# Two width-16 attentions: rounds of two pairs, four heads' scores on four strips, projection pieces in two slots a round

## The chip, the core and the metric

The kernel is one program on one core of a Trainium2 chip. The metric is the device time of one launch in microseconds, of which the median of three runs is given. TensorE (PE) multiplies, with its weight loads as PEld; VectorE (DVE), ScalarE (ACT) and GpSimd (POOL) compute; SyncE (SP) issues the transfers. The engines run side by side, each in its own fixed order, and wait for one another at semaphores.

## What is computed

Eight layers run after one another over x of 8 batches, 112 rows and 256 columns. The fifth and the seventh are the attentions of this change. Both have 16 heads of width 16 and 375 keys from the same context:

```python
# layer 5 (a2): _L2_xattn_ref
logits = jnp.einsum('bhqd,bhkd->bhqk', q, k) / jnp.sqrt(jnp.asarray(dh, q.dtype))
neg = (1.0 - mask.astype(q.dtype)) * -1000000000.0
attn = jax.nn.softmax(logits + neg[:, None, :, :], axis=-1)
attn = attn * group_prob[:, None, :, :]
out = jnp.einsum('bhqk,bhkd->bhqd', attn, v)     # then out @ wo_k + wo_b
# layer 7 (a3): _L3_xattn_ref
scores = jnp.einsum('bhqd,bhkd->bhqk', qh, kh) * SCALE
attn = jax.nn.softmax(scores, axis=-1)
out = jnp.einsum('bhqk,bhkd->bhqd', attn, vh)    # then out @ Wo.T + bo
# both: x = x + tanh(g) * attention(layernorm(x), ctx)
```

## The kernel before

Both layers are `narrow_attention`; a2 is called with `group` and `mask`, a3 without them and with `spare`, a helper that prepares the last layer's weights on idle engines. The 16 heads of a batch are eight pairs, numbered n = 8b + k over all eight batches b, so n runs from 0 to 63.

For each pair, TensorE makes the scores (`scores`), VectorE the negated maximum (`maximum`), ScalarE the exponents and their sum (`exponent`). In a2 GpSimd multiplies by the group (`regroup`). TensorE transposes the two probabilities (`turn`, two halves in banks 4 and 5), ScalarE copies the first half and VectorE the second (`copy_turned`), and for every two pairs TensorE multiplies with v (`weigh`, bank 6). The reciprocal of the sums (`invert`), its spreading to 128 columns on GpSimd (`expand`), TensorE's transpose of it (piece "I"), ScalarE's copy (`spread`) and VectorE's product (`move_out`) finish eight heads.

A head's scores use a strip of 32 of the array's 128 rows and a PSUM bank of their own, number j for strip j. A pair takes strips and banks 0 and 1 if n is even, 2 and 3 if odd. So the scores of pair n + 1 can be made while pair n is being read. Each score is three matmuls (high by high, high by low, low by high parts).

Between these steps TensorE makes the projections of the next batch, cut into pieces that all go to bank 7: K twice, V twice (twelve matmuls, then six), I twice and O once (the output projection of the batch before) for each batch, and Q at two places in all. The table `later` says after which n a piece stands, and `bank_free` makes it wait until the piece before it has been taken out of bank 7: K, V and O by VectorE (`evacuate`), I by ScalarE (`spread`), Q by both.

The order on every engine is written out by hand: one loop over n on each. Two other chains cross them. `high_context` (ScalarE) and `low_context` (GpSimd) split the context of batch b + 2 into parts before its K pieces; `high_queries` and `low_queries` do so with the queries of batch b + 1 before its first scores. GpSimd's loop is `regroup` for each n with these between.

## Time and profile before

| | us |
|---|---|
| median of three runs | 1427.72 |
| lowest, highest | 1417.14, 1428.33 |
| the profiled execution | 1423.97 |
| its span, first to last instruction | 1422.2 |
| TensorE busy in it | 1204.7 (85%) |
| VectorE, ScalarE, GpSimd busy | 860.9, 672.9, 532.3 |
| mean granted TensorE clock | 0.928 |

The profile is one execution. Busy shares over the whole span mix eight layers with different limits; for this change the stretches of the two attentions count. The steps before the first scores and after the last transpose stand outside them.

### The profile page before, as it was taken

The numbers are of one execution on the slowest core, as the hardware profiler recorded it, in microseconds if no ns is written. First come the engines' busy times: TensorE is split into PE (matmuls) and PEld (weight loads), VectorE is DVE, ScalarE is ACT, GpSimd is POOL, SyncE is SP. The second block draws the span as 40 slices with busy tenths as digits, with TensorE's granted clock in tenths as the row PEclk, the third lists the DMA queues.
The fourth block names the chain that finished last, engine by engine and source line by source line (L and its number), as shares of the span: only waits on it lengthen the run. The fifth ranks groups of instructions, "written<-read, shape, count | busy, mean of one in ns | idle before, by whom it ended". The sixth has DMA issues, their size and how long they took to land. (4 is left out here: it accounts for less than half of the span.)

```text
span 1422.2 us, 25398 instructions
## 1 busy us (share of the span) xinstructions
PE 1204.7 (85%) x9539; PEld 951.9 (67%) x9539; DVE 860.9 (61%) x1950; ACT 672.9 (47%) x1518; POOL 532.3 (37%) x537
## 2 busy tenths in 40 slices
PE   2999999999996887679999638999999428999967
PEld 2677777777774355456777538998888426777634
DVE  6664565555543336557787447667676356777686
ACT  3345543554541321256666316545554016766665
POOL 3355554565543000267887522001100232162132
PEclk9999999999997988779999559999999858999998
DMA  6000000000001052301100335565652152000000
GB/s 177 11 3 12 12 1 12 12 1 1 1 1 22 0 159 59 85 5 42 35 31 11 115 111 190 181 204 182 197 177 102 52 169 53 23 12 3 1 7 21
DMA packets 59929, 88.63 MB, mean 62 GB/s; under 512 B 8640, under 2 KB 49808, under 8 KB 59808
## 3 DMA queue, kind: packets, MB, share of 16 engines
q1 hardware_dynamic: 57696, 81.49, 18.5%
q0 software_dynamic: 2112, 5.51, 1.3%
q8 instruction: 78, 1.28, 0.4%
q14 instruction: 43, 0.35, 0.1%
HBM read 81.48 MB, written 5.51 MB: 61 GB/s over the span
## 5 line engine op out<-in xcount | busy, mean ns | idle before, releaser
L906 POOL TENSOR_SCALAR a_arena<-a_arena 112x487 f32<-112x487 f32 x128 | 192.7, 1517 | 175.3 <-DVE a_arena L1117 175.3
L1198 ACT ACTIVATE a_arena<-banks,a_arena 112x487 f32<-112x487 f32 x128 | 84.2, 663 | 192.1 <-DVE a_arena L1111 192.1
L1111 DVE TENSOR_REDUCE a_arena<-banks 112x2 f32<-112x974 f32 x64 | 75.0, 1172 | 101.1 <-PE banks L997 101.1
L93 PE MATMUL banks<-f_x_high,f_up_high 128*128 128x256 f32 x448 | 128.3, 286 | 3.6 <-DVE f_up_low L1981 2.2
L94 PE MATMUL banks<-f_x_low,f_up_high 128*128 128x256 f32 x448 | 127.9, 286 | 0.0
L95 PE MATMUL banks<-f_x_high,f_up_low 128*128 128x256 f32 x448 | 127.8, 285 | 0.0
L397 POOL TENSOR_TENSOR a_arena<-a_arena 112x375 f32<-112x375 f32 x128 | 114.7, 922 | 26.9 <-ACT a_arena L704 26.8
L513 PE MATMUL banks<-ident,a_arena 112*126 112x112 f32 x768 | 106.9, 277 | 12.0 <-POOL a_arena L397 10.0
L513 PEld LDWEIGHTS banks<-ident,a_arena 112*126 112x126 f32 x768 | 78.4, 145 | 46.6 <-issue 26.4
L2018 POOL DMA_INDIRECT f_arena<-f_rows,f_arena x28 | 32.1, 1145 | 194.7 <-PE banks L2051 175.2
L2162 DVE TENSOR_TENSOR f_arena<-banks,f_arena 128x512 f32<-128x512 f32 x56 | 38.5, 688 | 100.4 <-ACT f_arena L2141 100.4
L712 ACT COPY a_arena<-banks 126x336 f32<-126x336 f32 x128 | 55.9, 437 | 75.6 <-PE banks L513 75.6
L93 PEld LDWEIGHTS banks<-f_x_high,f_up_high 128*128 128x128 f32 x448 | 87.2, 195 | 4.2 <-issue 2.4
L93 PE MATMUL banks<-a_wv_high,a_kvT_high 128*122 128x512 f32 (+1 forms) x224 | 85.1, 380 | 4.8 <-DVE a_wv_low L605 2.9
L94 PEld LDWEIGHTS banks<-f_x_low,f_up_high 128*128 128x128 f32 x448 | 87.2, 195 | 0.0
L95 PEld LDWEIGHTS banks<-f_x_high,f_up_low 128*128 128x128 f32 x448 | 87.2, 195 | 0.0
L93 PE MATMUL banks<-a_kvT_high,a_wk_high 128*128 128x488 f32 (+1 forms) x192 | 82.7, 431 | 3.7 <-POOL a_kvT_low L891 3.5
L93 PE MATMUL banks<-f_down_high,f_h_high 128*128 128x256 f32 x224 | 64.4, 287 | 22.5 <-DVE f_arena L2175 22.5
L704 ACT ACTIVATE a_arena<-a_arena 112x375 f32<-112x375 f32 x128 | 77.0, 605 | 2.3 <-DVE a_arena L620 2.2
L95 PE MATMUL banks<-a_wv_high,a_kvT_low 128*122 128x512 f32 (+1 forms) x224 | 77.3, 345 | 0.0
L94 PE MATMUL banks<-a_wv_low,a_kvT_high 128*122 128x512 f32 (+1 forms) x224 | 77.3, 345 | 0.0
L704 ACT ACTIVATE a_arena<-banks,a_arena 112x375 f32<-112x375 f32 x128 | 72.8, 579 | 8.4 <-DVE a_arena L623 7.8
(331 smaller groups left out, 3312.6 us busy)
## 6 DMA issues: line engine op xcount, KB each, us to landing
f_arena<-in_L_ffn_w1T SPq DMA_DIRECT2D x14, 1024.0 KB, 5.8
f_arena<-in_L_ffn_w3T SPq DMA_DIRECT2D x14, 1024.0 KB, 4.8
f_arena<-in_L_ffn_w2T SPq DMA_DIRECT2D x14, 1024.0 KB
a_arena<-in_ctxT SPq DMA_DIRECT2D x24, 375.0 KB, 4.6
a_arena<-in_ctx SPq DMA_DIRECT2D x16, 375.0 KB
f_y<-f_arena SPq DMA_DIRECT2D x14, 256.0 KB, 5.0
a_arena<-in_L_xattn_Wkv SPq DMA_DIRECT2D x2, 1024.0 KB, 9.9
a_arena<-in_fside_BxSxS SPq DMA_DIRECT2D x8, 164.1 KB, 2.4
```

Of the source, the lines that this page charges most:

```text
L93: pe.matmul(out, sh, mh, start=start, stop=False)
L94: pe.matmul(out, sh, ml, start=False, stop=False)
L95: return pe.matmul(out, sl, mh, start=False, stop=stop)
L397: op = pool.tensor_tensor(z, z, gp[u], ALU.mult)
L513: mm = pe.transpose(psT[s][0:SZ, c * T:(c + 1) * T], prob[n % 4 * 2 + s][:, SZ * c:SZ * c + SZ], ident[0:T, 0:T])
L704: act.activation(prob[n % 4 * 2 + s][:, 0:KEYS], src, ACT.Exp, bias=negmax[:, n % 4, s:s + 1], scale=-1.0 if grouped else 1.0, accum_out=t ...
L712: act.copy(probT[n % 4 * 2].rearrange("k c t -> k (c t)"), psT[0][0:SZ, 0:NC * T]).then_inc(copied0, 1)
L906: pool.tensor_scalar(z, z, inv[:, n % 4, s:s + 1], None, ALU.mult).then_inc(p_ready, 1)
L1111: dve.tensor_reduce(negmax[:, n % 4, :], banks[0:T, 0:2, 0:KEYS], AX, ALU.max, negate=True).then_inc(max_ready, 1)
L1198: act.activation(prob[n % PR][s][:, 0:KEYS], banks[0:T, s, 0:KEYS], ACT.Exp, bias=negmax[:, n % 4, s:s + 1], accum_out=total[:, n % 4, s:s ...
L2018: pool.indirect_dma_start(rows[k % 2][:, h, :], None, rows_dram, bass.IndirectOffsetOnAxis(routing.token[:, h, k:k + 1], 0)).then_inc(rows ...
L2162: dve.tensor_tensor(gated[n % 2], ps3[n % 3], gel[n % 2], ALU.mult).then_inc(gated_done, 1)
```

## The change

Scores are made for two pairs (four heads) at once, on all four strips and banks: `scores(q)` for the pairs 2q and 2q + 1. Every loop goes in steps of two pairs, a round. On TensorE a round is: `turn` of the pair before, scores of the next round, a piece in the first slot, `turn`, `weigh`, a piece in the second slot. `scores` waits until all four maxima of the round before are there. VectorE, ScalarE and GpSimd are reordered to match. In a3 the maximum is made as in a2, with a `neg` of zeros, and the exponents read its result in SBUF, no longer the banks. K stands at k = 0 and 2 (before: 2 and 3), Q at n = 11 and 19 (before 8 and 16), `low_queries` at k = 4 (before 3); the spare work starts four pairs later.

```diff
--- before.py
+++ after.py
@@ -250,16 +250,16 @@
...
-    later = {8: ("Q", 0, 1), 16: ("Q", 1, 1)}
+    later = {11: ("Q", 0, 1), 19: ("Q", 1, 1)}
     for b in range(B):
         if b + 1 < B:
-            for k, kind, arg in ((2, "K", 0), (3, "K", 1), (6, "V", 0), (7, "V", 1)):
+            for k, kind, arg in ((0 if b else 3, "K", 0), (2 if b else 4, "K", 1), (6, "V", 0), (7, "V", 1)):
                 later[8 * b + k] = (kind, arg, b + 1)
...
     if spare is not None:
-        later[24] = ("M", 0, 0)
+        later[27] = ("M", 0, 0)
...
+        else:
+            neg = [m.sb("neg", [T, KEYS])] * 2
+        scored = [m.sb(f"scored{j}", [T, KEYS]) for j in range(4)]
+        spacers = m.sb("spacers", [T, 4])
...
+            else:
+                pool.memset(neg[0], 0.0).then_inc(neg_made, 1)
...
             pool.tensor_tensor(x[:], x[:], obs.unsqueeze(1).to_broadcast([T, B, D]), ALU.add).then_inc(biased, 1)
             for n in range(PAIRS + 2):
                 b, k = n // STEPS, n % STEPS
+                if n >= 4 and n % 4 == 0:
+                    expand(n // 4 - 1)
                 if grouped and n < PAIRS:
                     regroup(n)
-                if n >= 4 and n % 4 == 0:
-                    expand(n // 4 - 1)
                 if k == 1 and grouped and b + 1 < B:
                     negate_mask(b + 1)
                 if k == 5 and b + 2 < B:
                     low_context(b + 2)
-                if k == 3 and b + 1 < B:
+                if k == 4 and b + 1 < B:
                     low_queries(pool, b + 1)
-                if spare is not None and 26 <= n < 26 + spare.STEPS // 2:
+                if spare is not None and 30 <= n < 30 + spare.STEPS // 2:
                     for j in range(2):
-                        spare.gpsimd(pool, 2 * (n - 26) + j)
+                        spare.gpsimd(pool, 2 * (n - 30) + j)
...
-            def scores(n):
-                b, i, s = n // STEPS, n // 2 % 4, n % 2
-                u, g, e = b % 2, i // 2, i % 2
-                if n % STEPS == 0:
+            def scores(q):
+                b, g, e = q // 4, q // 2 % 2, q % 2
+                u = b % 2
+                if q % 4 == 0:
                     pe.wait_ge(piece_moved, moved(("K", 1, b))[0])
-                if n % STEPS == 0:
                     pe.wait_ge(q_low, b + 1)
-                if n > 1:
-
-                    pe.wait_ge(max_ready if grouped else exp_done, 2 * (n - 1))
+                if q:
+
+                    pe.wait_ge(max_ready, 4 * q)
                 for k, (a, z) in enumerate(((0, 0), (0, 1), (1, 0))):
-                    for h, j in heads_of(n):
+                    for j in range(4):
                         r = slice(32 * j, 32 * j + 32)
...
-            scores(1)
-            for n in range(LAST):
+            for n in range(0, LAST, 2):
+                if 0 < n <= PAIRS:
+                    turn(n - 1)
                 if n + 2 < PAIRS:
-                    scores(n + 2)
-                if n < PAIRS:
-                    turn(n)
-                if n >= 3 and n % 2 and n < PAIRS + 2:
-                    weigh((n - 3) // 2)
+                    scores(n // 2 + 1)
                 if n in later:
                     bank_free(n)
                     piece(later[n], 7)
+                if n < PAIRS:
+                    turn(n)
+                if 2 <= n < PAIRS + 2:
+                    weigh(n // 2 - 1)
+                if n + 1 in later:
+                    bank_free(n + 1)
+                    piece(later[n + 1], 7)
...
-                dve.wait_ge(s_ready, n + 1)
-                j, r = 2 * (n % 2), n % 4
...
-                else:
-                    dve.tensor_reduce(negmax[:, r, :], banks[0:T, j:j + 2, 0:KEYS], AX, ALU.max,
-                                      negate=True).then_inc(max_ready, 2)
+                dve.wait_ge(s_ready, n // 2 + 1)
+                b, j, r = n // STEPS, 2 * (n % 2), n % 4
+                if n % STEPS == 0 and (grouped or b == 0):
+                    dve.wait_ge(neg_made, b + 1)
+                if n > 1:
+                    dve.wait_ge(exp_done, 2 * (n - 1))
+                for s in range(2):
+
+                    dve.memset(spacers[:, j + s:j + s + 1], 0.0)
+                    dve.tensor_tensor_reduce(scored[j + s], banks[0:T, j + s, 0:KEYS], neg[b % 2], -1.0, LARGEST,
+                                             ALU.add, ALU.min, negmax[:, r, s:s + 1]).then_inc(max_ready, 1)
...
+            def taken(n):
+                if n in later and later[n][0] != "I":
+                    evacuate(later[n], 7)
+                    if later[n][0] == "O":
+                        dve.wait_ge(piece_moved, moved(later[n])[0])
+                        follow.row(dve, later[n][2])
+
             maximum(0)
-            for n in range(LAST + 1):
-                if n + 1 < PAIRS:
-                    maximum(n + 1)
+            maximum(1)
+            for n in range(0, LAST + 1, 2):
                 if 0 < n <= PAIRS:
                     copy_turned(n - 1)
-                if n >= 4 and n % 4 == 0 and n <= PAIRS:
-                    invert(n // 4 - 1)
+                taken(n - 1)
+                if n % 4 == 2 and n < PAIRS:
+                    invert(n // 4)
+                if n + 2 < PAIRS:
+                    maximum(n + 2)
                 if n >= 6 and n % 4 == 2 and n <= PAIRS + 2:
                     move_out(n // 4 - 1)
-                if n - 1 in later and later[n - 1][0] != "I":
-                    evacuate(later[n - 1], 7)
-                    if later[n - 1][0] == "O":
-                        dve.wait_ge(piece_moved, moved(later[n - 1])[0])
-                        follow.row(dve, later[n - 1][2])
+                taken(n)
+                if n < PAIRS:
+                    copy_turned(n)
+                if n + 3 < PAIRS:
+                    maximum(n + 3)
...
-                    act.wait_ge(max_ready, 2 * n + s + 1 if grouped else 2 * n + 2)
+                    act.wait_ge(max_ready, 2 * n + s + 1)
                     if n > 3:
                         act.wait_ge(t_ready, 2 * (n - 4) + s + 1)
-                    src = scored[j][:, 0:KEYS] if grouped else banks[0:T, j, 0:KEYS]
-                    act.activation(prob[n % 4 * 2 + s][:, 0:KEYS], src, ACT.Exp, bias=negmax[:, n % 4, s:s + 1],
-                                   scale=-1.0 if grouped else 1.0, accum_out=total[:, b % 2, h:h + 1]
+                    act.activation(prob[n % 4 * 2 + s][:, 0:KEYS], scored[j], ACT.Exp, bias=negmax[:, n % 4, s:s + 1],
+                                   scale=-1.0, accum_out=total[:, b % 2, h:h + 1]
...
-            for n in range(LAST + 1):
-                if n < PAIRS:
-                    exponent(n)
-                if spare is not None and n in (6, 9, 12, 14):
-                    spare.scalar(act, (6, 9, 12, 14).index(n))
+            exponent(0)
+            exponent(1)
+            for n in range(0, LAST + 1, 2):
                 if 0 < n <= PAIRS:
                     copy_turned(n - 1)
                 if n >= 6 and n % 4 == 2 and n <= PAIRS + 2:
                     spread(n // 4 - 1)
+                if n - 1 in later and later[n - 1][0] == "Q":
+                    odd(later[n - 1], 7)
+                if n + 2 < PAIRS:
+                    exponent(n + 2)
+                if n < PAIRS:
+                    copy_turned(n)
+                if n + 3 < PAIRS:
+                    exponent(n + 3)
+                if spare is not None and n in (6, 8, 12, 14):
+                    spare.scalar(act, (6, 8, 12, 14).index(n))
                 if n % STEPS == 4 and n // STEPS + 2 < B:
                     high_context(n // STEPS + 2)
-                if n - 1 in later and later[n - 1][0] == "Q":
-                    odd(later[n - 1], 7)
                 if n % STEPS == 2 and n // STEPS + 1 < B:
                     high_queries(n // STEPS + 1)
```

TensorE in a2 around the O piece of batch 2 (L466, L470), at k = 4 and after. L497 (L500 in the changed kernel) is `scores`, L513 (L516) `turn`, L532 (L535) `weigh`, L460 (L464) piece I, L93 here the first matmul of V. Before:

```order
L513 MATMUL banks<-ident,a_arena 126x112 x6
L466 MATMUL banks<-a_arena 112x256 x2
L497 MATMUL banks<-a_kT_high,a_q_high 112x376 x2
L497 MATMUL banks<-a_kT_low,a_q_high 112x376 x2
L497 MATMUL banks<-a_kT_high,a_q_low 112x376 x2
L513 MATMUL banks<-ident,a_arena 126x112 x6
L532 MATMUL banks<-a_arena 32x112 x12
L460 MATMUL banks<-ident,a_arena 128x112
L497 MATMUL banks<-a_kT_high,a_q_high 112x376 x2
L497 MATMUL banks<-a_kT_low,a_q_high 112x376 x2
L497 MATMUL banks<-a_kT_high,a_q_low 112x376 x2
L513 MATMUL banks<-ident,a_arena 126x112 x6
```

After:

```order
L500 MATMUL banks<-a_kT_high,a_q_high 112x376 x4
L500 MATMUL banks<-a_kT_low,a_q_high 112x376 x4
L500 MATMUL banks<-a_kT_high,a_q_low 112x376 x4
L470 MATMUL banks<-a_arena 112x256 x2
L516 MATMUL banks<-ident,a_arena 126x112 x6
L535 MATMUL banks<-a_arena 32x112 x12
L464 MATMUL banks<-ident,a_arena 128x112
L516 MATMUL banks<-ident,a_arena 126x112 x6
L500 MATMUL banks<-a_kT_high,a_q_high 112x376 x4
L500 MATMUL banks<-a_kT_low,a_q_high 112x376 x4
L500 MATMUL banks<-a_kT_high,a_q_low 112x376 x4
L93 MATMUL banks<-a_wv_high,a_kvT_high 126x256
```

Four heads stand in each score row, and between two score blocks there are two transposes and both slots. The V piece follows the scores directly, with I as the piece before it.

ScalarE in a2, batch 2, from k = 4 on. L704 (L714) is `exponent`, L712 (L722) `copy_turned`, L688 (L699) `high_context`, L733 (L743) `spread`, L729 the second half of Q. Before:

```order
L704 ACTIVATE a_arena<-a_arena 112x375 x2
L712 COPY a_arena<-banks 126x336
L688 CAST a_kvT_high<-a_arena 128x2x375
L704 ACTIVATE a_arena<-a_arena 112x375 x2
L712 COPY a_arena<-banks 126x336
L704 ACTIVATE a_arena<-a_arena 112x375 x2
L712 COPY a_arena<-banks 126x336
L733 COPY a_arena<-banks 128x112
```

After:

```order
L722 COPY a_arena<-banks 126x336
L729 ACTIVATE a_arena<-banks,a_arena 128x448
L714 ACTIVATE a_arena<-a_arena 112x375 x2
L722 COPY a_arena<-banks 126x336
L714 ACTIVATE a_arena<-a_arena 112x375 x2
L699 CAST a_kvT_high<-a_arena 128x2x375
L722 COPY a_arena<-banks 126x336
L743 COPY a_arena<-banks 128x112
L714 ACTIVATE a_arena<-a_arena 112x375 x2
```

Before, `high_context` stands between the exponents of k = 4 and k = 5, and `spread` behind the exponents of k = 6. Now both stand behind the exponents of k = 7, with a copy between them.

GpSimd in a2, batch 4, from k = 2 on. L397 (L399) is `regroup`, L363 (L365) `low_queries`, L388 (L390) `expand`, L371 (L373) `low_context`. Before:

```order
L397 TENSOR_TENSOR a_arena<-a_arena 112x375 x4
L363 TENSOR_TENSOR a_q_low<-a_arena,a_q_high 128x448
L397 TENSOR_TENSOR a_arena<-a_arena 112x375 x2
L388 COPY a_arena<-a_arena 112x128
L397 TENSOR_TENSOR a_arena<-a_arena 112x375 x2
L371 TENSOR_TENSOR a_kvT_low<-a_arena,a_kvT_high 128x2x375
L397 TENSOR_TENSOR a_arena<-a_arena 112x375 x6
```

After:

```order
L399 TENSOR_TENSOR a_arena<-a_arena 112x375 x4
L390 COPY a_arena<-a_arena 112x128
L399 TENSOR_TENSOR a_arena<-a_arena 112x375 x2
L365 TENSOR_TENSOR a_q_low<-a_arena,a_q_high 128x448
L399 TENSOR_TENSOR a_arena<-a_arena 112x375 x2
L373 TENSOR_TENSOR a_kvT_low<-a_arena,a_kvT_high 128x2x375
L399 TENSOR_TENSOR a_arena<-a_arena 112x375 x4
```

`expand` moved ahead of the products of k = 4, `low_queries` behind them; `low_context` stands behind those of k = 5 as before.

## Rows read from the trace of the kernel before

**Rows 1.** Busy us of each engine (and instructions) in stretches; then granted clock.
```profile
616.90:630.70 13.80, 8.65 (x38) 6.75 (x40) 4.77 (x21) 6.22 (x20) 12.84 (x13) 0.51 0.01 1
727.50:748.40 20.90, 20.76 (x233) 15.74 (x232) 16.61 (x71) 14.53 (x45) 17.82 (x22) 1.00 0.12 37
780.90:787.70 6.80, 6.80 (x48) 4.81 (x50) 2.44 (x12) 3.31 (x11) 4.80 (x7) 0.50 0.00 0
1285.20:1305.90 20.70, 20.70 (x233) 15.71 (x232) 15.85 (x31) 14.24 (x45) 3.21 (x4) 1.00 0.01 3
```

**Rows 2.** Timeline of TensorE in one batch of a2: start, length, engine, line.
```profile
706.68 0.36 PE L93 MATMUL banks<-a_wv_high,a_kvT_high 128*126 128x256 f32 x1
...
708.26 0.43 PE L497 MATMUL banks<-a_kT_high,a_q_high 32*112 32x376 f32 x2
...
715.96 0.79 PE L513 MATMUL banks<-ident,a_arena 112*126 112x112 f32 x6
716.52 0.42 PE L93 MATMUL banks<-a_kvT_high,a_wk_high 128*128 128x376 f32 x1
...
717.74 0.42 PE L497 MATMUL banks<-a_kT_high,a_q_high 32*112 32x376 f32 x2
...
722.70 1.12 PE L466 MATMUL banks<-a_arena 128*112 128x256 f32 x4
723.75 0.43 PE L497 MATMUL banks<-a_kT_high,a_q_high 32*112 32x376 f32 x2
...
724.45 0.79 PE L513 MATMUL banks<-ident,a_arena 112*126 112x112 f32 x6
725.18 0.78 PE L532 MATMUL banks<-a_arena 126*32 126x112 f32 x24
725.89 0.47 PE L460 MATMUL banks<-ident,a_arena 112*128 112x112 f32 x2
726.29 0.42 PE L497 MATMUL banks<-a_kT_high,a_q_high 32*112 32x376 f32 x2
```

**Rows 3.** Timeline of TensorE at the first scores of a3.
```profile
1176.90 0.44 PE L497 MATMUL banks<-a_kT_high,a_q_high 32*112 32x376 f32 x4
```

**Rows 4.** Timeline of VectorE in the same batch as rows 2.
```profile
716.08 0.55 DVE L620 CUSTOM_DVE_ANT_0 a_arena<-banks,a_arena 112x375 f32<-112x375 f32 x1 [0.15 <-issue]
...
717.02 0.50 DVE L630 COPY a_arena<-banks 126x336 f32<-126x336 f32 x1
717.84 0.61 DVE L580 TENSOR_SCALAR a_kT_high<-banks,a_arena 128x376 fp32r<-128x376 f32 x1 [0.32 <-PE banks L95]
...
719.02 0.55 DVE L620 CUSTOM_DVE_ANT_0 a_arena<-banks,a_arena 112x375 f32<-112x375 f32 x1
...
723.52 0.50 DVE L630 COPY a_arena<-banks 126x336 f32<-126x336 f32 x1
723.94 0.47 DVE L599 SCALAR_TENSOR_TENSOR x<-banks,tanh_g,x 112x256 f32<-112x256 f32 x1
```

**Rows 5.** Timeline of ScalarE in the same batch.
```profile
715.36 0.25 ACT L733 COPY a_arena<-banks 128x112 f32<-128x112 f32 x1 [0.87 <-PE banks L460]
715.51 0.57 ACT L727 CAST a_q_high<-a_arena 128x448 fp32r<-128x448 f32 x1
...
719.16 0.44 ACT L712 COPY a_arena<-banks 126x336 f32<-126x336 f32 x1 [0.38 <-PE banks L513]
719.50 0.82 ACT L688 CAST a_kvT_high<-a_arena 128x750 fp32r<-128x750 f32 x1
720.21 0.61 ACT L704 ACTIVATE a_arena<-a_arena 112x375 f32<-112x375 f32 x1
```

**Rows 6.** Timeline of GpSimd in the same batch.
```profile
718.50 1.16 POOL L363 TENSOR_TENSOR a_q_low<-a_arena,a_q_high 128x448 fp32r<-128x448 f32 x1
719.60 1.81 POOL L397 TENSOR_TENSOR a_arena<-a_arena 112x375 f32<-112x375 f32 x2
...
723.34 1.79 POOL L371 TENSOR_TENSOR a_kvT_low<-a_arena,a_kvT_high 128x750 fp32r<-128x750 f32 x1
```

More of the change, by code:

```diff
@@ L297, in narrow_attention @@
             neg = [m.sb(f"neg{u}", [T, KEYS]) for u in range(2)]
-            scored = [m.sb(f"scored{j}", [T, KEYS]) for j in range(4)]
-            spacers = m.sb("spacers", [T, 4])
+        else:
+            neg = [m.sb("neg", [T, KEYS])] * 2
+        scored = [m.sb(f"scored{j}", [T, KEYS]) for j in range(4)]
+        spacers = m.sb("spacers", [T, 4])
         psT, psO, psP = [banks[:, 4 + j, :] for j in range(2)], banks[:, 6, :], banks[:, 7, :]
@@ L608, in maximum @@
             def maximum(n):
-                dve.wait_ge(s_ready, n + 1)
-                j, r = 2 * (n % 2), n % 4
-                if grouped:
-                    b = n // STEPS
-                    if n % STEPS == 0:
-                        dve.wait_ge(neg_made, b + 1)
-                    if n > 1:
-                        dve.wait_ge(exp_done, 2 * (n - 1))
-                    for s in range(2):
-                        dve.memset(spacers[:, j + s:j + s + 1], 0.0)
-                        dve.tensor_tensor_reduce(scored[j + s], banks[0:T, j + s, 0:KEYS], neg[b % 2], -1.0, LARGEST,
-                                                 ALU.add, ALU.min, negmax[:, r, s:s + 1]).then_inc(max_ready, 1)
-                else:
-                    dve.tensor_reduce(negmax[:, r, :], banks[0:T, j:j + 2, 0:KEYS], AX, ALU.max,
-                                      negate=True).then_inc(max_ready, 2)
+                dve.wait_ge(s_ready, n // 2 + 1)
[8 more added lines that the diff above has]
+                                             ALU.add, ALU.min, negmax[:, r, s:s + 1]).then_inc(max_ready, 1)
             def copy_turned(n):
@@ L725, in high_queries @@
                 if b > 1:
-                    act.wait_ge(s_ready, STEPS * (b - 1))
+                    act.wait_ge(s_ready, STEPS // 2 * (b - 1))
                 act.copy(q_parts[b % 2][0][:], qm[:, :, :, b * T:(b + 1) * T]).then_inc(q_high, 1)
```

## Prediction

> **What bounds the kernel now.** I read the stretches first, then the order on TensorE inside one batch, then the other engines over the same microseconds. The change touches only the two width-16 attentions, called a2 (with group and mask) and a3 below. They run from about 614 and 1177 us. A middle batch of a2 lasts 20.90 us, of which TensorE is busy 20.76. One of a3 lasts 20.70 and TensorE never idles in it [rows 1]. So TensorE is the bound, and a block taken off its queue is worth its full length until another engine becomes the bound. The reader should look at that second candidate in the same rows: GpSimd is busy 17.82 us of a batch in a2, VectorE 16.61 (a2) and 15.85 (a3), ScalarE 14.53 and 14.24. The gap above the next engine is only 3 us.
>
> By starts on TensorE [rows 2]: a score block S (three passes, two heads) takes 0.70 us, the transposes of a pair T 0.73, the weighing W of two pairs 0.71, pieces K 1.22, V (twelve matmuls) 1.58, O 1.05, I 0.40; V with six matmuls I put at 0.9. A T before K is 0.56, before W 0.73: what follows in another shape of the array costs some 0.15 more. K and V were followed by S and are now followed by T, so I take 0.15 off each of them: K 1.07, V 1.43 and 0.75. Before, a batch is 8 S, 8 T, 4 W and seven pieces.
>
> **What is removed.** Four heads now share one S. Do four strips cost more than two? At the head of a3 the first two score blocks already follow each other with nothing between, and the trace merges them: a pass over four strips is 0.44 us against 0.42 for two [rows 2, 3]. So four S of 0.70 leave each batch: 2.8 us. 31 rounds in each of two attentions have a block to drop, some 62 x 0.70 = 43 us. That is what the change would give if nothing else held TensorE.
>
> The Trainium skill ("TensorE: Matmul & The Clock Gate", Measured speedup vs the span model) gives four row strips a speedup of 3.07, not 4, that is 1.3 times the time of one strip. By that, about 0.15 us would be added to each of the 62 rounds, 9 us in all. The row on four strips disagrees, and the row decides.
>
> **What is added: one set of score banks.** Before, S for the next pair went to two banks while VectorE read the other two. Now S takes all four, so it waits until both maxima of the round before are done. I lay out one round from the start of S at 0, with VectorE in its new order: maximum, evacuation of the piece, copy of T, maximum.
> - First maximum starts 0.82 after S; a pair of maxima takes 0.94; a K piece is taken up 1.32 after its start and costs 1.18; a copy 0.42 [rows 4].
> - Round with K and no delay: maxima to 1.76, K (started at 0.70) taken up at 2.02, done 3.20, copy 3.62, maxima 4.56, and with 0.14 for the last maximum's accumulator and the signal (an estimate) S at 4.70. TensorE alone would need 0.70 + 1.07 + 0.73 + 0.71 + 0.73 = 3.94. VectorE is the bound there.
> - Round with O and I: TensorE 0.70 + 1.05 + 0.73 + 0.71 + 0.40 + 0.73 = 4.32, VectorE 4.2. Round with both V: TensorE 0.70 + 1.43 + 0.73 + 0.71 + 0.75 + 0.73 = 5.05.
> Sum 4.70 + 4.70 + 4.32 + 5.05 = 18.8 against 20.8. So a third of what the blocks and shapes save already goes to VectorE's chain.
>
> The Trainium skill ("TensorEngine Tiling (Array Packing)", PSUM Bottleneck) warns of this: tiling speeds up the matmuls, not the emptying of PSUM, which can take over. By that rule alone a batch would end near 18.8; the round with K agrees with it, the V round does not.
>
> **What is moved: ScalarE and the one piece bank.** All pieces use bank 7, so a piece waits until the one before has been taken out. I is now in the second slot of a round (k = 1 and 5) and K or V in the first slot of the next (k = 2 and 6). I is taken out by ScalarE (`spread`), which now stands behind the two exponents of the pair whose maximum came last, and behind a copy. An exponent costs 0.61, a copy 0.34, `spread` 0.25 [rows 5]. Last maxima start 1.08 before S; first exponent 0.58 later, two take 1.22, copy 0.34, `spread` 0.25: bank 7 is free 1.33 after S, where the piece could go at 0.70.
> - Round k = 2: K starts at 1.33 instead of 0.70, VectorE takes it up at 2.65, then 1.18, 0.42 and 1.08 for the next S: 5.3 instead of 4.7.
> - Round k = 6: in the new order `high_context` (0.71, [rows 5]) also stands ahead of that copy and `spread`, so V starts at 2.04: 2.04 + 1.43 + 0.73 + 0.71 + 0.75 + 0.73 = 6.4 instead of 5.05.
> - Round k = 0: V's second half is taken out only after the copy of T, so K starts some 0.25 late: 4.9.
> Sum 4.9 + 5.3 + 4.3 + 6.4 = 20.9 in a3, against 20.7: +0.2. The score blocks saved are waited for again.
>
> **a2 has GpSimd too.** It multiplies each probability (`regroup`, 1.81 a pair), and T waits for it. `low_queries` (1.16) now stands behind `regroup` of k = 4 and needs ScalarE's `high_queries`, which comes after the exponents of pair k = 5. GpSimd is through with k = 4 about 2 us before that, and waits. `low_context` (1.79 [rows 6]) stands behind `regroup` of k = 5 and needs `high_context`, now behind the exponents of k = 7: another 1.5 us of waiting. Add 3.5 to the 17.8 it is busy and GpSimd needs 21.3, more than TensorE had. Laid out: T of k = 5 waits 0.6, T of k = 6 waits 1.3 behind `low_context`, and the other waits of these rounds partly overlap: about 22.3 us a batch against 20.9, +1.4.
>
> **The small parts.** In the first batch the clock is half (0.51 in [rows 1]) and a score block costs about 1.2, so dropping two there is worth more: -2.0 in a3; in a2 GpSimd's late start and `low_context` keep all but 0.5. Batch 6 has no `high_context`: -0.5 in each. Batch 7 has no K or V; a round of 3.55 before stays near 3.6 by ScalarE and VectorE, and only its O round gains: -0.8 in each. In a3 the maximum is now two instructions, 0.94 a pair, in place of one reduction of about the same, already in the layout. The new `memset` of `neg` lies ahead of the first scores beside a GpSimd that waits: nothing. The Q pieces move one slot and the spare weight work four pairs later; I cost both at zero, because the spare work only needs to end before a3 does; between -1 and +1 a batch for the two batches with Q.
>
> **Sum.** a2: 5 x 1.4 - 0.5 - 0.5 - 0.8 = +5.2. a3: 5 x 0.2 - 2.0 - 0.5 - 0.8 = -2.3. Together +3 us on the profiled execution, 1423.97, so 1427. The median of the runs shown is 3.75 above that execution: 1430.7, and I say 1430. About 1% (14 us) is what a measurement of this kernel can tell from no change. An error of 0.7 us in one batch's layout repeats 14 times and makes 10 us, so 1418 to 1442 is this case's own range.
>
> **Rivals.**
> *Only VectorE's chain binds (faster).* If ScalarE runs early enough that bank 7 is free when asked for, and GpSimd never waits long, a batch is 18.8: 12 x 2.0 + 3 at the ends = -27 from the median, 1401. For it: ScalarE has 6 us of slack a batch and GpSimd 3. Against it: their order, in which the wanted copy stands behind exponents that are released last. 0.28, of which 0.03 for the whole 43 us (1385).
>
> **Chances.** Forecast's case 0.50, faster 0.28, slower 0.22. The range takes in the faster rival's 1401 and half of the slower one: 1396 to 1452.
>
> **What would show it.** Score rows with x4 and a pass near 0.44: removed work right. TensorE waits before K at k = 2 and before V at k = 6, of 0.6 and 1.3 us, released by ScalarE's copy of I: the bank. S waiting on VectorE's maximum in K rounds: the chain. In a2, T waiting for GpSimd's product, with GpSimd idle until ScalarE's two casts. Batches of 20.9 in a3 and 22.3 in a2. I am wrong if a batch of a3 is below 20, if a2's batches are not longer than a3's, or if the clock falls inside the middle batches.

## The result, and the profile after

The changed kernel took 1441.08 us (median of 10 runs, 1432.09 to 1446.03), the kernel before, on the same chip, 1424.88 (10 runs, 1415.70 to 1437.97). The ratio is 1.0116, 95% interval 1.0087 to 1.0145: slower by 16 us. The range (1396 to 1452) holds it. The forecast was 1430, that is 0.2% above the median that it started from; the measured time is inside its own band of 1418 to 1442 by only 0.9 us, and as a ratio it is slower by more than the 1% that the forecast's case allowed. The profiled execution took 1440.02.

The head of the profile of the changed kernel: its span, then the busy time of the engines.

```profile
span 1438.3 us, 25718 instructions
PE 1166.2 (81%) x9539; PEld 929.8 (65%) x9539; DVE 865.9 (60%) x2270; ACT 676.5 (47%) x1518; POOL 532.1 (37%) x538
```

TensorE is busy 38.5 us less than before, and the span is 16.1 us longer. (Between the second profiles of both kernels, experiments 9 and 10, it is 46.1 us; 43 were predicted.) So the work was removed, and TensorE waits for more than it saved. One batch of a2, one of a3, and 3.4 us inside a3's second batch, columns as in [rows 1]:

```profile
684.17:706.91 22.74, 18.42 (x230) 14.16 (x230) 16.12 (x70) 14.40 (x44) 18.08 (x22) 1.00 0.12 34
1275.15:1296.26 21.11, 18.07 (x231) 14.16 (x231) 16.62 (x71) 14.46 (x45) 15.56 (x19) 1.00 0.07 20
1215.50:1218.90 3.40, 3.29 (x12) 2.93 (x12) 1.24 (x3) 1.69 (x6) 0.00 (x0) 0.50 0.00 0
```

In [rows 1] TensorE idled 0.14 us of a batch of a2 and not at all in a3. Now it idles 4.3 and 3.0. No other engine is full either, so these are waits in a circle of engines. The timeline of TensorE in that batch of a3 shows them: start, length, and in brackets the idle time ahead and who ended it.

```profile
1279.53 0.43 PE L500 MATMUL banks<-a_kT_high,a_q_high 32*112 32x376 f32 x4
...
1280.54 0.45 PE L93 MATMUL banks<-a_kvT_high,a_wk_high 128*128 128x376 f32 x1 [0.23 <-DVE a_arena L597]
...
1284.58 0.43 PE L500 MATMUL banks<-a_kT_high,a_q_high 32*112 32x376 f32 x4 [0.32 <-DVE a_arena L625]
...
1285.90 0.44 PE L93 MATMUL banks<-a_kvT_high,a_wk_high 128*128 128x376 f32 x1 [0.55 <-ACT a_arena L743]
...
1289.93 0.43 PE L500 MATMUL banks<-a_kT_high,a_q_high 32*112 32x376 f32 x4 [0.39 <-DVE a_arena L625]
...
1294.31 0.43 PE L500 MATMUL banks<-a_kT_high,a_q_high 32*112 32x376 f32 x4 [0.20 <-DVE a_arena L625]
...
1296.26 0.38 PE L93 MATMUL banks<-a_wv_high,a_kvT_high 128*126 128x256 f32 x1 [1.17 <-ACT a_arena L743]
```

Each of these score rows is x4 and 0.43 long, as [rows 3], and a whole block of four strips takes 0.70 by starts, as one of two strips did. K follows the scores by 1.01 and 1.32, V by 1.95 us, where 0.70 would do. The last two are released by L743, `spread`. ScalarE over the last of these waits:

```profile
1293.72 0.61 ACT L714 ACTIVATE a_arena<-a_arena 112x375 f32<-112x375 f32 x1 [0.70 <-DVE a_arena L625]
...
1294.33 0.59 ACT L714 ACTIVATE a_arena<-a_arena 112x375 f32<-112x375 f32 x1
...
1294.92 0.80 ACT L699 CAST a_kvT_high<-a_arena 128x750 fp32r<-128x750 f32 x1
1295.63 0.43 ACT L722 COPY a_arena<-banks 126x336 f32<-126x336 f32 x1
1295.96 0.25 ACT L743 COPY a_arena<-banks 128x112 f32<-128x112 f32 x1
```

Two exponents, `high_context` (L699), a copy and then `spread`, which frees bank 7. In a2 the same cast holds up GpSimd, which waits 1.66 us for it and only then multiplies the pair whose transpose TensorE is waiting for. GpSimd first, then TensorE:

```profile
728.93 1.80 POOL L373 TENSOR_TENSOR a_kvT_low<-a_arena,a_kvT_high 128x750 fp32r<-128x750 f32 x1 [1.66 <-ACT a_kvT_high L699]
730.69 1.78 POOL L399 TENSOR_TENSOR a_arena<-a_arena 112x375 f32<-112x375 f32 x2
```

```profile
727.33 0.80 PE L516 MATMUL banks<-ident,a_arena 112*126 112x112 f32 x6 [0.66 <-POOL a_arena L399]
...
732.53 0.79 PE L516 MATMUL banks<-ident,a_arena 112*126 112x112 f32 x6 [1.43 <-POOL a_arena L399]
```

A batch is measured from its first V matmul to that of the next batch. The first stretch starts at the first scores, the last one ends at the start of the last O matmul. The profiled executions compare so (us; "predicted" is the prediction's difference):

| | before | after | difference | predicted |
|---|---|---|---|---|
| a2, to the first V | 25.61 | 25.25 | -0.4 | -0.5 |
| a2, two batches with Q | 46.31 | 50.16 | +3.9 | +2.8 |
| a2, three middle batches | 62.60 | 67.95 | +5.4 | +4.2 |
| a2, batch 6 | 20.89 | 21.87 | +1.0 | -0.5 |
| a2, end | 29.38 | 27.67 | -1.7 | -0.8 |
| a3, to the first V | 21.87 | 22.02 | +0.2 | -2.0 |
| a3, two batches with Q | 44.98 | 50.23 | +5.3 | +0.4 |
| a3, three middle batches | 62.15 | 63.24 | +1.1 | +0.6 |
| a3, batch 6 | 20.68 | 20.39 | -0.3 | -0.5 |
| a3, end | 23.12 | 23.61 | +0.5 | -0.8 |
| both attentions | 357.6 | 372.4 | +14.8 | +2.9 |

The unchanged layers make up the rest of 16.1.

One row of the table can't be taken at its word. The end of a2 holds 11.0 us at half clock in the profile before and 9.4 in the one after. In experiments 8 and 9, which run the old function there, it holds 3.4 and takes 25.95 and 25.94, not 29.38. The profile before, that of experiment 9, and the changed kernel:

```profile
769.30:798.68 29.38, 25.90 (x275) 19.07 (x273) 15.84 (x71) 14.49 (x47) 18.08 (x22) 0.81 0.00 1
```

```profile
765.28:791.22 25.94, 22.46 (x274) 17.07 (x273) 15.99 (x71) 14.49 (x47) 18.07 (x22) 0.93 0.00 1
```

```profile
773.99:801.66 27.67, 22.41 (x276) 17.26 (x272) 16.89 (x73) 14.27 (x45) 18.42 (x23) 0.83 0.00 1
```

The changed kernel takes 27.67 there in both its profiles. So its end of a2 is 1.7 us shorter against one profile of the kernel before and 1.7 longer against the other.

### The profile page after: what moved, and what is told of

The parts are those of the page before. It is cut to its first block and busy times, and to the rows that moved or that the text cites. A ratio compares the mean times of both kernels' runs of the same rounds, so it can differ in the third digit from the quotient of the medians.

```text
span 1438.3 us, 25718 instructions
## 1 busy us (share of the span) xinstructions
PE 1166.2 (81%) x9539; PEld 929.8 (65%) x9539; DVE 865.9 (60%) x2270; ACT 676.5 (47%) x1518; POOL 532.1 (37%) x538
## 5 line engine op out<-in xcount | busy, mean ns | idle before, releaser
L714 ACT ACTIVATE a_arena<-a_arena 112x375 f32<-112x375 f32 x256 | 153.8, 602 | 92.8 <-DVE a_arena L625 90.6
L625 DVE CUSTOM_DVE_ANT_0 a_arena<-banks,a_arena 112x375 f32<-112x375 f32 x256 | 130.8, 546 | 8.7 <-issue 5.3
L93 PE MATMUL banks<-f_x_high,f_up_high 128*128 128x256 f32 x448 | 128.6, 287 | 3.6 <-DVE f_up_low L1997 2.2
L516 PE MATMUL banks<-ident,a_arena 112*126 112x112 f32 x768 | 103.7, 272 | 21.3 <-POOL a_arena L399 13.7
L399 POOL TENSOR_TENSOR a_arena<-a_arena 112x375 f32<-112x375 f32 x128 | 114.1, 919 | 5.5 <-ACT a_arena L714 4.5
L516 PEld LDWEIGHTS banks<-ident,a_arena 112*126 112x126 f32 x768 | 84.7, 147 | 37.2 <-POOL a_arena L399 19.2
L93 PE MATMUL banks<-a_wv_high,a_kvT_high 128*122 128x512 f32 (+1 forms) x224 | 86.0, 384 | 18.7 <-ACT a_arena L743 13.7
L2178 DVE TENSOR_TENSOR f_arena<-banks,f_arena 128x512 f32<-128x512 f32 x56 | 38.5, 688 | 103.0 <-ACT f_arena L2157 103.0
L93 PE MATMUL banks<-a_kvT_high,a_wk_high 128*128 128x488 f32 (+1 forms) x192 | 83.8, 436 | 16.6 <-ACT a_arena L743 7.6
L93 PEld LDWEIGHTS banks<-f_x_high,f_up_high 128*128 128x128 f32 x448 | 87.6, 195 | 4.2 <-issue 2.4
L632 DVE COPY a_arena<-banks 126x336 f32<-126x336 f32 x128 | 64.2, 501 | 43.1 <-PE banks L516 43.1
L93 PE MATMUL banks<-f_down_high,f_h_high 128*128 128x256 f32 x224 | 65.4, 292 | 22.5 <-DVE f_arena L2191 22.5
```

Of the source, the lines that this page charges most:

```text
L93: pe.matmul(out, sh, mh, start=start, stop=False)
L399: op = pool.tensor_tensor(z, z, gp[u], ALU.mult)
L516: mm = pe.transpose(psT[s][0:SZ, c * T:(c + 1) * T], prob[n % 4 * 2 + s][:, SZ * c:SZ * c + SZ], ident[0:T, 0:T])
L625: dve.tensor_tensor_reduce(scored[j + s], banks[0:T, j + s, 0:KEYS], neg[b % 2], -1.0, LARGEST, ALU.add, ALU.min, negmax[:, r, s:s + 1]).t ...
L632: dve.tensor_copy(probT[n % 4 * 2 + 1].rearrange("k c t -> k (c t)"), psT[1][0:SZ, 0:NC * T]).then_inc(copied1, 1)
L714: act.activation(prob[n % 4 * 2 + s][:, 0:KEYS], scored[j], ACT.Exp, bias=negmax[:, n % 4, s:s + 1], scale=-1.0, accum_out=total[:, b % 2, ...
```

## The experiments

Ratios are to the kernel before on the same chip. Batch lengths are from the V piece of one batch to that of the next, as above; "Q" marks the two with a Q piece.

**1. Piece I in a bank of its own.** I goes to unused columns of bank 6; K and V wait only for pieces that VectorE takes out.

```diff
-                    mm = pe.matmul(ps[:, 0:T], invx[gg % 2], ident[0:T, 0:T], start=True, stop=True)
+                    if gg:
+                        pe.wait_ge(i_moved, gg)
+                    mm = pe.matmul(psI, invx[gg % 2], ident[0:T, 0:T], start=True, stop=True)
...
-                before = [later[j] for j in sorted(later) if j < n]
+                if later[n][0] == "I":
+                    return
+                before = [later[j] for j in sorted(later) if j < n and later[j][0] != "I"]
...
-                act.copy(iT, psP[:, 0:T]).then_inc(i_moved, 1)
+                act.copy(iT, psI).then_inc(i_moved, 1)
```

> The changed kernel, with piece I written beside the weighing's output in bank 6 and so no longer in bank 7: no K or V piece waits for ScalarE's copy of I. My theory (the waits for bank 7 eat the gain): TensorE's wait before K at k = 2 (0.6 us) and before V at k = 6 (1.25 us) are gone. a3's batches go from 21.07 to about 19.0 us, a2's from 22.7 to about 21.5, since there low_context still comes late: 20 to 25 us less than the changed kernel, a ratio to the kernel before of about 0.995 to 1.0. Rival, VectorE's chain alone binds: the K round stays at 5.3 and only the V round gains, at most 9 us. Rival, the clock: the time stays at 1.012.

Measured: 1430.62 us, ratio 1.0052 (1.0016 to 1.0087). a3's middle batches take 19.26 to 19.57, so the bank was worth 1.8 us a batch there (1.5 in the last of the three). In a2 the expectation (21.5) was missed: they take 24.19, 23.12 and 22.20. The first two hold 3.4 us at half clock each; the third, at full clock, is 0.5 shorter than in the changed kernel. TensorE reaches the transpose sooner and waits longer for GpSimd, 1.81 in the second of them and in the first 2.69, where it was 1.43:

```profile
691.08 0.80 PE L519 MATMUL banks<-ident,a_arena 112*126 112x112 f32 x6 [2.69 <-POOL a_arena L400]
```

So in a2 GpSimd, and what GpSimd waits for, leaves little of this gain. The ratio was expected at 0.995 to 1.0 and came out above.

**2. Both casts early.** `high_context` and `high_queries` stand ahead of the exponents of the next pair.

```diff
                     odd(later[n - 1], 7)
+                if n % STEPS == 4 and n // STEPS + 2 < B:
+                    high_context(n // STEPS + 2)
+                if n % STEPS == 2 and n // STEPS + 1 < B:
+                    high_queries(n // STEPS + 1)
                 if n + 2 < PAIRS:
                     exponent(n + 2)
...
-                if n % STEPS == 4 and n // STEPS + 2 < B:
-                    high_context(n // STEPS + 2)
-                if n % STEPS == 2 and n // STEPS + 1 < B:
-                    high_queries(n // STEPS + 1)
```

> The changed kernel, with high_context and high_queries on ScalarE moved ahead of the exponents of their round instead of behind them. My theory: V at k = 6 starts 1.3 after its scores instead of 1.94, in a3 0.6 us less a batch; in a2 GpSimd's low_context and low_queries no longer wait, and the transposes at k = 5 and k = 6 with them: 1.5 us less a batch. About 4 + 10 = 14 us less than the changed kernel, ratio to before about 1.002. If only VectorE's chain or the clock count, nothing changes (1.012).

Measured: 1423.23 us, ratio 0.9985 (0.9950 to 1.0019). Middle batches are 20.35 in both attentions: 0.7 less in a3 (0.6 expected) and 2.3 less in a2 (1.5 expected). In the middle batches the two attentions become equal once GpSimd need not wait.

**3. Both edits.**

> Both edits: I in bank 6 and the two ScalarE casts ahead of the exponents. My theory: what is left is VectorE's chain in the K rounds. Batches of 18.8 to 19.2 in a3 and 19.0 to 19.8 in a2, 35 to 40 us less than the changed kernel, ratio to before 0.985 to 0.99. If VectorE's chain alone had been the cause, this is no better than 1.005.

Measured: 1404.23 us, ratio 0.9858 (0.9801 to 0.9916). All middle batches are 19.27, within 0.02. Together the two give more than their sum: 36.9 us off the changed kernel, against 10.5 and 17.9 by the medians, and 37, 9 and 19 by the ratios. The traces show two reasons for it, without dividing it between them: in a2 the first edit alone shortens a batch by 0.5 and no more, and with it alone five of the six batches of a2 between V pieces hold 3.4 us at half clock, with both none.

**4. VectorE's maxima first.** The changed kernel, with `maximum(n + 3)` ahead of the pieces and the copy.

```diff
+                if n + 3 < PAIRS:
+                    maximum(n + 3)
                 if n >= 6 and n % 4 == 2 and n <= PAIRS + 2:
                     move_out(n // 4 - 1)
-                taken(n)
                 if n < PAIRS:
                     copy_turned(n)
-                if n + 3 < PAIRS:
-                    maximum(n + 3)
+                taken(n)
```

> The changed kernel, with VectorE making both maxima of a round one after the other, ahead of the copy of the first transposes and of taking out the piece. The scores' wait for VectorE is gone from the K rounds. Rival (VectorE's chain alone binds): a batch falls by 0.6 + 1.2 and the kernel by 25 us, to 0.994 of the kernel before. My theory: the exponents come earlier too, so ScalarE reaches its copy of I before or just after the scores and the bank waits shrink as well; the piece is taken out of bank 7 some 1.4 us later and the next piece waits for that. 15 to 30 us less. It alone can't tell the two theories apart; e1 does.

Measured: 1435.97 us, ratio 1.0102 (1.0063 to 1.0141). The scores no longer wait for VectorE, but the pieces do, since they are taken out of bank 7 later:

```profile
1298.05 0.47 PE L464 MATMUL banks<-ident,a_arena 112*128 112x112 f32 x2 [1.05 <-DVE a_kT_low L589]
...
1307.29 0.47 PE L464 MATMUL banks<-ident,a_arena 112*128 112x112 f32 x2 [0.57 <-DVE x L606]
```

The last two middle batches of a3 gain 0.4 us, those of a2 0.4 to 0.5, and the first of a3 loses 0.9. Expected were 15 to 30 us; 5 came, by the medians, with intervals of the ratios that overlap. VectorE's chain is one side of the circle, bank 7 another; to loosen one alone moves the wait.

**5. All three edits.**

> I in bank 6, the two ScalarE casts early, and both maxima first on VectorE in every round. My theory of what is left in e3 (a batch of 19.27 in both attentions): scores wait 0.5 to 0.7 us for VectorE in the two K rounds. Here these waits go, but the pieces are taken out later, and the next piece waits for bank 7 (V's second half for its first by 0.6 us, more at k = 0): about 18.8 to 19.6 a batch, a ratio of 0.983 to 0.99. If VectorE's chain is not what is left, nothing changes or the batch gets longer.

Measured: 1404.38 us, ratio 0.9852 (0.9770 to 0.9934). Middle batches 18.82 (19.95 in the one of a3 that holds the spare piece M), 0.45 better than in experiment 3, but those with Q 22.6 instead of 21.5 to 22.0, and nothing is left of it in the time.

**6. Experiment 3 with the maxima first only where a K piece stands.** In rounds with O or V the order of the changed kernel stays; before k = 0 the second V piece is taken out ahead of the copy.

```diff
+                early = later.get(n, "K")[0] == "K"
+                if early and n + 3 < PAIRS:
+                    maximum(n + 3)
...
-                taken(n)
+                if not early:
+                    taken(n)
                 if n < PAIRS:
                     copy_turned(n)
-                if n + 3 < PAIRS:
+                if early:
+                    taken(n)
+                elif n + 3 < PAIRS:
                     maximum(n + 3)
```

> As e3, with both maxima first only in the rounds whose first piece is K, and V's second half taken out ahead of the copy of the transposes at k = 0. My theory: the waits of the scores (0.5 and 0.7 us) and of K at k = 0 (0.3 us) go, and a batch is 18.0 to 18.6, 10 to 17 us less than e3: ratio 0.975 to 0.98. If the chain is bound by VectorE's total work instead (16.6 us busy in 19.27), it stays within 3 us of e3.

Measured: 1402.70 us, ratio 0.9836 (0.9734 to 0.9939). Two middle batches, columns as before:

```profile
714.47:732.76 18.29, 17.44 (x234) 14.23 (x231) 16.52 (x70) 14.35 (x46) 17.10 (x21) 1.00 0.15 42
1264.96:1283.22 18.26, 17.40 (x235) 14.23 (x231) 16.47 (x70) 14.36 (x46) 10.86 (x12) 1.00 0.01 3
```

TensorE idles 0.9 us of a batch. The layout was met in the middle batches (18.0 to 18.6 expected; 19.46 in the one with M), the time was not: 10 to 17 us less than experiment 3 were expected, and it is 1.5 less. The batches between V pieces together are 5.6 us shorter; those with Q are 22.0, up to 0.5 longer than in experiment 3. The rest is inside the spread of executions, 1393.57 to 1410.57 here.

**7. Only `high_context` early.**

> The changed kernel with high_context alone moved ahead of the exponents; high_queries stays late. It splits e2. My theory: in a3 the same as e2, 20.4 a batch, since only high_context stands ahead of the copy of I at k = 6. In a2 the wait of the transposes at k = 6 (1.3 us, behind low_context) goes, the one at k = 5 (0.5 to 0.8 us, behind low_queries) stays: 21.0 a batch against 20.35 in e2 and 22.7 in the changed kernel. Ratio to before about 1.002.

Measured: 1420.55 us, ratio 0.9972 (0.9932 to 1.0012). a3's middle batches 20.35, a2's 20.44 to 21.07 (20.4 and 21.0 expected). This one cast accounts for nearly all of experiment 2: 1.7 to 2.3 us of a batch in a2 and 0.7 in a3.

**8. The change in a3 alone.** a2 keeps the function of before.

> The change in a3 alone; a2 runs the function of before. My theory, from the traces: a2 lost 10 us and a3 6, so this is 6 to 7 us slower than before, 1.0045, and a2's part is larger because only there does GpSimd stand between exponents and transposes. If the loss comes from anything that both share (bank 7, the maxima), the two halves are equal, 1.006.

Measured: 1433.38 us, ratio 1.0050 (1.0012 to 1.0087). Its interval is too wide to tell the expectation's two cases, 1.0045 and 1.006, apart. By the first two profiles a3 lost 6.7 us of the 14.8 and a2 8.1. Both attentions lose time; how it divides stays open, since the end of a2 alone moves by 3.4 between profiles (above).

**9 and 10. The kernel before and the changed one once more,** one execution each, for the spread of the layers that nothing changed.

> The kernel before once more, for a second profile of it. From a3's last scores to the end the first profile has 80.7 us and every kernel with the change 86 to 92, of which the last layer, whose code is the same, makes 4 us or more at a half clock. If the change causes that, this profile has 80 to 82 again; if it is the spread between executions, 84 to 90.

> The changed kernel once more, for the same purpose. The batches stay at 22.5 and 21.1 us (order and waits are fixed); the part after a3's last scores is again between 86 and 92 if the change causes it, and anywhere from 80 to 92 if it does not.

Measured: 1431.71 and 1439.32 us. After the last O of a3 the kernel before takes 72.5 us in the first profile and 79.7 in this one:

```profile
1349.70:1422.20 72.50, 50.54 (x226) 30.91 (x224) 54.88 (x140) 44.17 (x66) 22.22 (x25) 0.88 0.05 14
```

```profile
1349.90:1429.60 79.70, 54.80 (x227) 32.39 (x225) 54.93 (x140) 44.28 (x66) 22.16 (x25) 0.80 0.04 12
```

VectorE's and ScalarE's work is the same within 0.2 us, the granted clock 0.88 and 0.80. The changed kernel takes 77.0 and 77.1, between the two. (Counted from the last scores, as the expectation does, it is 80.7 and 87.8 before, 88.0 and 88.1 after.) So the last layer's longer time is no effect of the change. The two attentions together take 357.6 and 355.5 us before, 372.4 and 376.5 after: 14.8 to 21.0 more, in line with the 16 of the medians. So the loss lies inside the attentions, as far as two profiles of each kernel can tell.

**11. The spare Abs behind the copy of I.**

```diff
                     odd(later[n - 1], 7)
+                if spare is not None and n in (8, 10, 14, 16):
+                    spare.scalar(act, (8, 10, 14, 16).index(n))
...
-                if spare is not None and n in (6, 8, 12, 14):
-                    spare.scalar(act, (6, 8, 12, 14).index(n))
```

> The changed kernel with one move on ScalarE in a3: the four Abs instructions of the spare work (1.04 us and 0.19 each) stand behind the copy of I and the second half of Q of the next round, not behind the exponents ahead of them. In the changed kernel one ends just before the copy that frees bank 7 at n = 10 and another before the one at n = 14, and the first Q batch of a3 takes 24.7 to 25.3 us at full clock, the second 22.7 to 23.4. If those Abs are what makes the first one long, K at n = 10 starts 0.5 to 0.7 after the scores end instead of 1.6, V at n = 14 1.2 instead of 2.2, and the first Q batch falls to 22.7 to 23.4. If Q itself makes it long, it stays at 24.7 or more. The whole time should fall by 1 to 2 us, less than one execution can show.

Measured: 1440.52 us, one execution. In the changed kernel an Abs of 1.04 stood just ahead of the copy and `spread`, and K waited 1.59 (the V after it 2.21):

```profile
1213.96 1.04 ACT L2268 ACTIVATE qw_arena<-qw_arena 128x1024 bf16<-128x1024 f32 x1
...
1215.00 0.42 ACT L722 COPY a_arena<-banks 126x336 f32<-126x336 f32 x1
1215.32 0.24 ACT L743 COPY a_arena<-banks 128x112 f32<-128x112 f32 x1
```

```profile
1215.61 0.68 PE L93 MATMUL banks<-a_kvT_high,a_wk_high 128*128 128x376 f32 x1 [1.59 <-ACT a_arena L743]
```

Here the same K and the V after it wait no longer than in a middle batch:

```profile
1211.09 0.44 PE L93 MATMUL banks<-a_kvT_high,a_wk_high 128*128 128x376 f32 x1 [0.55 <-ACT a_arena L743]
...
1223.72 0.39 PE L93 MATMUL banks<-a_wv_high,a_kvT_high 128*126 128x256 f32 x1 [1.18 <-ACT a_arena L743]
```

The first Q batch is 24.89 us with 3.4 of them at half clock, against 26.81 with as many in the changed kernel. At full clock it would be near 23.4 (an estimate from the 1.55 us that such a stretch cost in experiment 10, below), as the second one is (23.42). So the Abs made it 1.9 longer. Experiment 2 agrees: with the Abs in its old place its two Q batches in a3, both at full clock, are 24.72 and 22.70.

**12. Experiment 6 with the Abs moved.**

> The kernel of the sixth experiment (piece I in bank 6, both context casts early, maximum first in K rounds) with the four Abs moved as in the eleventh. There no piece waits for the copy of I, so the Abs only delay a copy of T. If bank 7 was the whole of their cost, nothing changes: the first Q batch of a3 stays at 22.0, as a2's, and the ratio is 0.984 again. If a late copy of T costs too, it falls by up to 1 us. Either way within 0.980 to 0.988.

Measured: 1404.74 us, ratio 0.9879 (0.9852 to 0.9906). The Q batches stay at 22.0. Where no piece waits for the copy of I, the place of the Abs costs nothing. The layouts of experiments 3, 5, 6 and 12 all end between 1402.7 and 1404.7 us, 1.2 to 1.6% below the kernel before; their intervals overlap and none of them can be called best.

## Why the prediction was right or wrong

**Right: TensorE was the bound, four strips cost as two.** The x4 rows, the block of 0.70 and the 38.5 us less of busy time show it. The rival of strips that don't overlap falls.

**Right: the waits and their makers.** K at k = 0, K at k = 2 and V at k = 6 were put at 0.95, 1.33 and 2.04 behind the scores, and came at 1.01, 1.32 and 1.95. A middle batch of a3 was put at 20.9 and took 21.1. In a2 the transpose of k = 5 was to wait 0.6 and that of k = 6 1.3; they wait 0.66 and 1.43, and a middle batch takes 22.5 to 22.7 against 22.3. Experiment 1 shows the cause in a3 (the piece that ScalarE holds in bank 7), experiments 2 and 7 the one in a2 (the casts behind the exponents), and experiment 3 that with both undone the kernel is faster than before. The 0.14 that the prediction put between the last maximum and the next scores as an estimate is what one K round shows: the maximum reads its result from 1284.44 on and the scores start at 1284.58.

**Partly right: VectorE's chain.** The 18.8 that it was to give alone is what experiment 5 measured (18.82). The rival in which only this chain binds, given 0.28, needed bank 7 and GpSimd to be free in time, and they were not. One reading in the prediction's own sum is off: VectorE's chain takes 2 x 0.76 of the 3.55 us that a batch would save by TensorE alone, over two fifths, where it says a third.

**Wrong: the small parts.** The direction was right and the size was not: +2.9 us were predicted for the two attentions and +14.8 came. The time lies in the range because the range was wide. Of the 11.9 us between the predicted and the measured difference of the two attentions, the six middle batches make 1.7 and the two Q batches of a2 1.1, from a layout 0.2 to 0.5 too short. (A K piece before a transpose takes 1.14 and V 1.52, not 1.07 and 1.43, since the other shape behind them costs 0.07 or 0.08 less and not 0.15; a transpose takes 0.67, not 0.73.) The rest lies where no round had been laid out:
- "The Q pieces move one slot and the spare weight work four pairs later; I cost both at zero" failed in a3: +5.3 us for its two Q batches against +0.4 predicted. Experiment 11 shows what was missed: the Abs that moved from n = 9 to n = 8 stands ahead of the copy that frees bank 7 at n = 10, and the one at n = 12 ahead of the copy for n = 14. The prediction had asked only whether the spare work ends in time, not what is queued behind it. Of the 5.3 us these Abs are about 1.9 and the clock about 1.5 (below); the rest is 0.9 for each of the two batches, where a middle batch lost 0.4, so Q or the spare work beside it costs some 0.5 a batch more. In a2, without spare work, the Q batches lost 1.9 and 2.0, about as much as the middle ones, so there Q itself was rightly put at zero.
- "Batch 6 has no `high_context`: -0.5 in each" failed in a2: +1.0, a term mis-sized by 1.5. `low_context` of the batch before still stands in this stretch, and the first transpose after the V piece waits for GpSimd behind it. So six batches hold this wait, not five:

```profile
752.12 0.38 PE L93 MATMUL banks<-a_wv_high,a_kvT_high 128*126 128x256 f32 x1 [0.56 <-ACT a_arena L743]
...
754.99 0.79 PE L516 MATMUL banks<-ident,a_arena 112*126 112x112 f32 x6 [1.19 <-POOL a_arena L399]
```

  With `high_context` early (experiment 7) the same batch takes 20.80, not 21.87, and with both casts early (experiment 2) 20.36. In a3, without GpSimd, it was -0.3.
- "-2.0 in a3" for the first batch failed: +0.2. With 10.2 us at half clock in both profiles it took 21.87 and 22.02. The kernel before took 23.35 in experiment 9, with 13.7 at half clock. By these two the clock moves it 0.42 us for each us at half, so with 6.8 it would take about 20.4 (an estimate). The same function as in the changed kernel took 20.49, 20.49 and 20.56 with 6.8 (experiments 8, 10 and 11). So nothing of the -2.0 can be seen. The prediction took the two score blocks off and counted none of the waits of its own rounds in this batch. They are there: at the same 6.8 the stretch takes 19.80 with both casts early (experiment 2) and 19.26 with the bank as well (experiment 3).
- "-0.8 in each" for batch 7 failed in a3: +0.5. The transposes wait for ScalarE's copy, once for 1.65, where the longest such wait in the profile before is 1.13. The stretch is 23.6 in experiments 3 and 7 too, so neither bank 7 nor the casts are the cause, and it stays open. In a2 the table has -1.7, but there the half clock of the profile before decides (above), and the term is neither shown nor refuted. The row of 1.65:

```profile
1355.78 0.77 PE L516 MATMUL banks<-ident,a_arena 112*126 112x112 f32 x6 [1.65 <-ACT a_arena L722]
```

The chances: slower by over 1% had 0.22, and the measured 1.16%, with an interval from 0.87 to 1.45, lies astride that bound. "GpSimd's waits in a2 and ScalarE's in a3 each come out 1 us a batch longer" was the rival nearest to it; what happened was 0.2 to 0.5 us more in the batches that had been laid out and up to 4 in the few that had not. Of the signs of being wrong that the prediction names, a batch of a3 below 20 and batches of a2 no longer than a3's did not appear. The third did once: in experiment 10 the clock fell inside one middle batch of a2 and one of a3.

## What to carry to other kernels

When the bound engine is relieved by work that shares a buffer with others, lay out the round for every engine that has to hand the buffer back, and look at the order there: where two casts stood, and in which bank one small piece stood, decided between 1.2% slower and 1.4% faster; an Abs in the wrong place cost another 1.9 us. Loosen all the sides of such a circle at once, or at least judge an edit only together with the others; one of them alone (experiment 1 in a2, experiment 4) can show little. And lay out the first, the last and the odd batches too: cheap auxiliary work that moves by one slot can land in front of a release.

## What the hardware showed beyond that

**With more waiting, often half clock inside the batches.** In its two profiles the kernel before has no half clock in its 24 batches between V pieces. The changed kernel has one such stretch of 3.4 us in a2 and one in a3; in experiment 10 one in a2, and in the first three batches of a3 17 us together; the same function in experiment 8 has 6.8 in a3. Two neighbouring batches of a3 in experiment 10, the first holding one of them:

```profile
1251.74:1274.36 22.62, 19.70 (x232) 15.77 (x233) 17.11 (x75) 14.44 (x45) 3.47 (x5) 0.92 0.07 19
1274.36:1295.43 21.07, 18.04 (x230) 14.13 (x231) 16.62 (x71) 14.44 (x45) 15.60 (x19) 1.00 0.07 20
```

It costs 1.55 us, nearly half of 3.4. In a2 of the same execution a batch with one took 22.81, where the same batch at full clock took 22.48 in the first profile and in experiment 11, and its neighbours 22.72 and 22.73. So where GpSimd sets the pace, a slower TensorE costs 0.1 to 0.3 us and not 1.55. Experiments 2, 3, 5, 6 and 12, with less waiting, had none in these batches, and experiment 1, with the longest waits, had five in a2. But experiment 4 had none either, with batches about as long as the changed kernel's, and experiment 7 had one, in a Q batch of a3. So the waiting goes with the half clock in most runs and does not decide it alone; no experiment was made on it. The half clock of the rival "the clock falls" did appear, at a fraction of its price.

**Unchanged layers differ by more than the change's measure.** From the last O of a2 to the first scores of a3 only the `memset` of `neg` was added, and the kernel before took 378.2 and 384.4 us there in two executions, with 94.8 and 105.8 us at half clock; the changed one took 380.2 and 379.4. One profile against another can't show an effect of a few us in this kernel: the two spans of the kernel before differ by 7.4. The stretch between two V pieces can, since at full clock it repeats within 0.1 us from one profile of a kernel to the other.
